# A state-space and attention block on one core: TensorE folds two steps' states together in every second step

## The chip, the cores and the metric

The kernel runs on one core of one Trainium2 chip. The metric is device microseconds of a whole launch, lower is better. The profiler recorded one execution instruction by instruction. In this document PE is TensorE (matmuls), DVE is VectorE, ACT is ScalarE, POOL is GpSimd and SP is the queue that issues the DMAs.

## The reference

Input x is 4 sequences of 512 tokens with 256 channels. The first half is a state-space layer, the second an attention and MLP block on the 64 best scored tokens of each sequence. The part that matters here is the scan of the first half, shortened:

```python
deltaA  = exp(einsum('bld,dn->lbdn', delta, A))        # n = 16 states per channel
deltaBu = einsum('bld,bln->lbdn', delta * u, Bm)
def step(h, inp):
    dA, dBu, c = inp
    h = dA * h + dBu                                   # along the 512 tokens
    return h, einsum('bdn,bn->bd', h, c)               # sum over the 16 states
y   = scan(...) + u * D
out = (y * silu(r)) @ W_out + xs                       # r, xs, u, delta, Bm, C come from x
x1  = layernorm(x + out);  then scores, top 64 tokens, attention + MLP on them, layernorm
```

## The kernel before

The loop that the change touches has 64 **steps**, t = 0 to 63: 16 for each of the 4 sequences (b = t // 16). A step takes one pair of 64-channel halves for two of the 16 states. Its work goes through five engines, which run their own programs and meet at semaphores:

- ACT `make_z` (L1009) multiplies delta times u by B, in four chunks of tokens for each two steps: chunks 0 to 2 are written in an even step for the next two, chunk 3 at the start of the following odd step. ACT `make_decay` (L1019) makes the decays.
- PE `turn_bu` (L522) transposes a quarter of that into one of three banks: four matmuls a call, two calls a step. I call them the first and the second turn of a step. PE issues the turns of step t+1 while it is in its own step t. The first turn of an even step reads newly made chunks, so it waits for ACT's chunk 3; this wait falls into PE's odd steps.
- DVE `scan` (L1171) runs the recurrence, two scans a step, into `state`, which has room for four steps. The first scan of step t waits until step t-4 has been folded (`summed`).
- POOL `weigh` (L1545) multiplies the state by C.
- PE `add_states` (L657) is the **fold**: two 128x512 matmuls with the constant matrix `fold` that sum the two states of a step into bank 4 (even steps) or bank 5 (odd steps). It waits for `weighed`, and for the first fold of a sequence into a bank also for `y_taken`: DVE must have read the finished y out of that bank (L1223).

Around these, each step has pieces of the sequence after (**fronts**: transposes of x, convolution in four quarters `cv0a` to `cv1d`, gate `r0`/`r1`, `dt`, `bc`, `cr`/`dl`, `du`) and of the sequence before (**tails**: `o0`, `o1`, scores `sb`, ranks, selection `pf`, gather `ga`, angles `cs`). The tables `FRONT_AT` and `TAIL_AT` say in which step each piece stands, on all engines. PE's order in a step is: first turn of t+1, fold, tails, second turn of t+1, fronts. ACT copies the result of many pieces out of PSUM and waits for them in its own order: `dt` (in steps with t%16 = 4) and the last convolution quarters stand in even steps, `r0`, `r1` (t%16 = 3), `bc` (5), `o0` (3), `du` (13) and `cs` (t = 47) in odd steps.

Of the kernel before, what the change touches and what calls it, by code (L numbers as in the profile page):

```python
# [90 lines left out]
def block_kernel(nc, x, W_in, conv_w, conv_b, W_x, W_dt, b_dt, A_log, D, W_out, w_router, wq, bq, wk, bk, wv, bv,  # L91
# [45 lines left out]
    def tails(t):  # L137

        b, n = t // NST, t % NST
        return [(b - 1, piece) for piece in TAIL_AT.get(n, ())] if b >= 1 else []  # L140

    def fronts(t):


        late = {"cv1b": -16, "cv1c": -15, "cv1d": -14}
        return [(b, piece) for b in range(B - 1, 0, -1) for off in sorted(FRONT_AT) for piece in FRONT_AT[off]
                if b * NST + (late.get(piece, off) if b == 1 else off) == t and not (b == 1 and piece in EARLY)]

    def norms(t):

        return NORM_AT.get(t - (B - 1) * NST)
# [47 lines left out]
    with ExitStack() as ctx:  # L199
# [320 lines left out]
        def _(pe):  # L520
# [114 lines left out]
            def turn_bu(u):  # L635

                g, k = u // 4, u % 4
                if u >= NBU:
                    pe.wait_ge(scanned, u - NBU + 1)
                for c in range(C):  # L640
                    if k == 0:
                        if g == 0 and c >= C // 2:
                            pe.wait_ge(z_dve, 2 * (c - C // 2 + 1))
                        else:
                            pe.wait_ge(z_act, z_count(g, c))
                    mm = turn(bank[BU_BANK[u % NBU]][:, c * P:(c + 1) * P],
                              zed[:, g % NZ, c, k].rearrange("p n d -> p (n d)"))
                mm.then_inc(bu_filled, 1)

            def add_states(t):  # L650

                b, m, h = t // NST, t % NST // 2, t % 2
                if m == 0 and b >= 1:
                    pe.wait_ge(y_taken, KD * (b - 1) + h + 1)
                pe.wait_ge(weighed, t + 1)
                for j in range(2):
                    mm = pe.matmul(bank[Y_BANK[h]][j * P // 2:(j + 1) * P // 2, :], fold[:], state[:, t % NH, j, :],  # L657
                                   start=(m == 0), stop=(m == NPAIR - 1))
                mm.then_inc(summed, 1)

            def rows_to_T(name, count):

                p = name[1]
                wait_free(pe, name)
                pe.wait_ge(h_ready, count)
                for k in range(KD):
                    mm = turn(at(name)[:, k * P:(k + 1) * P], h_rows[:, p, k * P:(k + 1) * P])
                fill_done(name, mm)
# [68 lines left out]
            for t in range(B * NST):  # L737
                if 2 * t + 2 < NU:
                    turn_bu(2 * t + 2)
                if t >= 2:  # L740
                    add_states(t - 2)
                for b, piece in tails(t):
                    tail(b, piece)
                if 2 * t + 3 < NU:
                    turn_bu(2 * t + 3)
                for b, piece in fronts(t):
                    front(b, piece)
                if norms(t) == "ht":
                    rows_to_T(("h1T", 0), 1)
# [907 lines left out]
```

## Time and profile before

| what | us |
|---|---|
| median of 3 runs (lowest, highest) | 519.88 (516.26, 520.61) |
| the profiled execution's own time | 519.67 |
| its span, first to last instruction | 517.9 |
| its loop of 64 steps on DVE, start of the first scan to the last | 62.9 to 368.4 |

The span and the time of the execution differ by 1.8 us, which lies outside of the recorded instructions. Busy shares of the span are PE 82%, ACT 65%, DVE 58% and POOL 49%, so no engine is full, and the loop is some three fifths of the span.

### The profile page before, as it was taken

The page shows a single profiled execution, that of the slowest core. Times are in us where ns is not written, and L with a number is a line of the kernel's source. Part 1 is how long each engine was busy: PE and PEld are TensorE (multiplying, and loading weights), DVE is VectorE, ACT ScalarE, POOL GpSimd, SP SyncE. Part 2 cuts the span into 40 slices and gives each one's busy share as a digit, 9 for nine tenths or more (in the row PEclk, how much of TensorE's full clock was granted, in tenths as well). Part 3 has the DMA queues.
Part 4 walks back from the last instruction along what each step waited for, and adds up shares of the span by engine and source line. Part 5 has one row for each costly group of instructions (what it writes and reads, how often), then busy time and mean ns, then how long its engine had stood idle before and what let it go on. Part 6 is the DMA issues. An engine that isn't in the chain of part 4 may idle for free.

```text
span 517.9 us, 6511 instructions
## 1 busy us (share of the span) xinstructions
PE 426.4 (82%) x2021; PEld 255.3 (49%) x2021; DVE 299.1 (58%) x600; ACT 334.5 (65%) x736; POOL 253.7 (49%) x230
## 2 busy tenths in 40 slices
PE   5988888878979869888958688877796888999992
PEld 3432443343445334544524454533384576887881
DVE  0301554558564549855655986789668257553365
ACT  4235689795769795577797386996186298543242
POOL 2001074469555659557667757695654144332012
PEclk9998999989999979899997697989998799999997
DMA  8001700104100102301000412662120000000003
GB/s 249 13 0 46 197 25 22 41 1 120 45 22 20 41 2 51 96 28 34 20 21 2 124 41 103 209 234 107 50 113 1 2 0 1 1 2 1 1 33 130
DMA packets 18710, 29.11 MB, mean 56 GB/s; under 512 B 2698, under 2 KB 10676, under 8 KB 18420
## 3 DMA queue, kind: packets, MB, share of 16 engines
q1 hardware_dynamic: 18676, 28.70, 17.8%
q8 instruction: 16, 0.26, 0.2%
q14 instruction: 18, 0.15, 0.1%
HBM read 22.27 MB, written 2.23 MB: 47 GB/s over the span
## 4 chain that ended last, share of the span: by engine, by line
PE 36%; ACT 15%; issue 9%; DVE 8%; POOL 7%; POOLq 0%; DVEq 0%; ACTq 0%
PE bank L522 6%; ACT loop_buf L1009 6%; PE bank L657 5%; POOL state L1545 4%; PE bank L538 4%; ACT front_a L1019 3%; PE bank L833 3%; DVE state L1171 3%; PE bank L809 3%; PE bank L603 2%; ACT state L1043 2%; ACT state L1044 1%; PE bank L841 1%; PE bank L800 1%; PE bank L612 1%
## 5 line engine op out<-in xcount | busy, mean ns | idle before, releaser
L1171 DVE TENSOR_TENSOR_SCAN state<-front_a,bank 128x512 f32<-128x512 f32 x128 | 151.2, 1209 | 102.2 <-PE bank L522 62.3
L522 PE MATMUL bank<-ident,loop_buf 128*128 128x128 f32 x512 | 90.9, 299 | 40.1 <-ACT loop_buf L1009 33.3
L522 PEld LDWEIGHTS bank<-ident,loop_buf 128*128 128x128 f32 x512 | 63.0, 149 | 109.5 <-issue 37.3
L1009 ACT ACTIVATE loop_buf<-copy,b_rows 128x256 f32<-128x256 f32 x252 | 105.3, 496 | 0.1
L1545 POOL TENSOR_TENSOR state<-state,c_own 128x1024 f32<-128x1024 f32 x32 | 75.2, 2359 | 50.3 <-DVE state L1171 50.3
L1545 POOL TENSOR_TENSOR state<-state,front_a 128x1024 f32<-128x1024 f32 x32 | 79.9, 2510 | 37.9 <-DVE state L1171 37.9
L1019 ACT ACTIVATE front_a<-loop_buf,a_neg 128x512 f32<-128x512 f32 x128 | 84.4, 712 | 10.9 <-DVE state L1171 9.9
L657 PE MATMUL bank<-state,fold 128*64 128x512 f32 x256 | 75.5, 671 | 10.2 <-POOL state L1545 6.1
L538 PE MATMUL bank<-front_c,conv_raw 128*128 128x512 f32 x128 | 60.4, 603 | 2.9 <-ACT front_b L884 1.2
L538 PEld LDWEIGHTS bank<-front_c,conv_raw 128*128 128x128 f32 x128 | 22.9, 195 | 23.7 <-issue 20.4
L1562 POOL TENSOR_TENSOR loop_buf<-state 128x256 f32<-128x256 f32 x24 | 17.8, 742 | 30.3 <-DVE state L1316 30.3
L884 ACT ACTIVATE front_b<-bank,vec 128x512 f32<-128x512 f32 x16 | 10.9, 682 | 31.5 <-PE bank L538 28.4
L884 ACT ACTIVATE copy<-bank 128x512 f32<-128x512 f32 x20 | 11.4, 594 | 28.2 <-PE bank L522 20.6
L681 PE MATMUL bank<-h,copy 128*128 128x128 f32 x192 | 24.5, 280 | 3.2 <-DVE state L1312 2.3
L681 PEld LDWEIGHTS bank<-h,copy 128*128 128x128 f32 x192 | 22.5, 192 | 6.0 <-DVE state L1312 3.6
L1312 DVE SCALAR_TENSOR_TENSOR state<-bank,vec,cosT 128x128 f32<-128x128 f32 x48 | 14.5, 344 | 18.8 <-ACT state L1044 18.6
L1519 POOL TENSOR_TENSOR copy<-front_c,front_b 128x1024 f32<-128x1024 f32 x4 | 8.0, 1998 | 35.0 <-ACT front_b L884 35.0
L657 PEld LDWEIGHTS bank<-state,fold 128*64 128x64 f32 x256 | 13.5, 144 | 22.7 <-POOL state L1545 9.1
L1043 ACT ACTIVATE state<-bank,vec 64x128 f32<-64x128 f32 x48 | 17.4, 364 | 10.3 <-PE bank L681 9.5
L1189 DVE TENSOR_SCALAR front_c<-front_b 128x512 f32<-128x512 f32 x2 | 0.9, 429 | 32.2 <-ACT front_b L948 32.1
L1044 ACT ACTIVATE state<-bank,vec 64x128 f32<-64x128 f32 x48 | 17.3, 360 | 0.6
L603 PE MATMUL bank<-w_out_s,gT 128*128 128x256 f32 x64 | 17.1, 390 | 0.4 <-POOL gT L1574 0.4
(197 smaller groups left out, 681.6 us busy)
## 6 DMA issues: line engine op xcount, KB each, us to landing
front_a<-c_stage SPq DMA_DIRECT2D x32, 128.0 KB, 2.9
c_own<-c_stage SPq DMA_DIRECT2D x32, 128.0 KB, 2.9
loop_buf<-front_b SPq DMA_DIRECT2D x32, 128.0 KB, 2.4
copy<-in_L_attn_x SPq DMA_DIRECT2D x4, 512.0 KB, 4.9
front_b<-in_L_ffn_wo SPq DMA_DIRECT2D x1, 2048.0 KB, 9.0
copy<-in_L_ffn_wq SPq DMA_DIRECT2D x1, 2048.0 KB, 9.6
out<-loop_buf SPq DMA_DIRECT2D x3, 512.0 KB, 2.9
conv_raw<-in_L_attn_conv_w SPq DMA_DIRECT2D x2, 512.0 KB, 3.7
```

Source lines behind the costliest of these rows:

```text
L522: return pe.transpose(dst, src, ident[:])
L538: mm = pe.matmul(at(name)[:], conv_x[:, k, i, o * P:(o + 1) * P], xT[:, i, k:k + L], start=(j == 0), stop=(j == TAPS * KD - 1))
L603: mm = pe.matmul(t[:, i * DM:(i + 1) * DM], gT[:, k, cols], w_out_s[:, k, :], start=(k == 0), stop=(k == KD - 1))
L657: mm = pe.matmul(bank[Y_BANK[h]][j * P // 2:(j + 1) * P // 2, :], fold[:], state[:, t % NH, j, :], start=(m == 0), stop=(m == NPAIR - 1))
L681: mm = pe.matmul(at(name)[:, i * P:(i + 1) * P], w_qk[:, k, head * P:(head + 1) * P], hT[:, k, p * P:(p + 1) * P], start=(k == 0), stop=(k ...
L884: drain_done(name, act.activation(dst, at(name)[:] if src is None else src, func, **kw))
L1009: act.activation(zed[:, g % NZ, c, :, i, :], du_rows[b % 2][:, c, :].rearrange("p (k d) -> p k d", k=2 * KD), ACT.Copy, scale=b_rows[:, b ...
L1019: act.activation(decay[:, u % NDA, :], delta_wide[:, b % 2, k, :], ACT.Exp, scale=a_neg[:, k, m:m + 1]).then_inc(decay_made, 1)
L1043: act.activation(qk_swap[0:mid, i0 % NQK, i, :], src[mid:, :], ACT.Identity, bias=vec[mid:, w:w + 1])
L1044: last = act.activation(qk_swap[mid:, i0 % NQK, i, :], src[0:mid, :], ACT.Identity, bias=vec[0:mid, w:w + 1])
L1171: dve.tensor_tensor_scan(state[:, t % NH, j, :], decay[:, u % NDA, :], bank[BU_BANK[u % NBU]][:], 0.0, ALU.mult, ALU.add).then_inc(scanned, 1)
L1545: pool.tensor_tensor(state[:, t % NH], state[:, t % NH], c_wide[g % NCW].unsqueeze(1).to_broadcast([P, 2, L]), ALU.mult).then_inc(weighed, 1)
```

## The change

PE calls `add_states` in odd steps alone, twice: first for step t-3, then for step t-2. The fold of an odd step stays in the PE step where it was; the fold of an even step is issued one PE step later, in front of it. The two folds behind the loop (steps 62 and 63) stay. No other engine's program changes.

```diff
             for t in range(B * NST):
                 if 2 * t + 2 < NU:
                     turn_bu(2 * t + 2)
-                if t >= 2:
+                if t % 2 and t >= 3:
+                    add_states(t - 3)
                     add_states(t - 2)
                 for b, piece in tails(t):
                     tail(b, piece)
```

Below, on PE in steps 5 and 6 (the first turn of step 6, in bank 0, is the first row; `bc` is L569 and `dl` is L586). Before:

```order
L522 MATMUL bank0<-ident,loop_buf 128x128 x4
L657 MATMUL bank5<-state,fold 64x512 x2
L522 MATMUL bank2<-ident,loop_buf 128x128 x4
L569 MATMUL bank6<-copy1,w_x_s 32x512 x2
L522 MATMUL bank3<-ident,loop_buf 128x128 x4
L657 MATMUL bank4<-state,fold 64x512 x2
L522 MATMUL bank0<-ident,loop_buf 128x128 x4
L574 MATMUL bank7<-ident,bcT 128x32 x4
```

After:

```order
L522 MATMUL bank0<-ident,loop_buf 128x128 x4
L657 MATMUL bank4<-state,fold 64x512 x2
L657 MATMUL bank5<-state,fold 64x512 x2
L522 MATMUL bank2<-ident,loop_buf 128x128 x4
L569 MATMUL bank6<-copy1,w_x_s 32x512 x2
L522 MATMUL bank3<-ident,loop_buf 128x128 x4
L522 MATMUL bank0<-ident,loop_buf 128x128 x4
L574 MATMUL bank7<-ident,bcT 128x32 x4
```

In the odd step two folds now stand between the first turn and everything behind it; in the even step none does. Next, on PE in steps 18 to 20, where the first folds of the second sequence stand (L603 and L607 are `o0`, L560 are `r0` and `r1`). Before:

```order
L522 MATMUL bank3<-ident,loop_buf 128x128 x4
L657 MATMUL bank4<-state,fold 64x512 x2
L522 MATMUL bank0<-ident,loop_buf 128x128 x4
L522 MATMUL bank2<-ident,loop_buf 128x128 x4
L657 MATMUL bank5<-state,fold 64x512 x2
L603 MATMUL bank6<-w_out_s,gT 128x256 x2
```

After:

```order
L522 MATMUL bank0<-ident,loop_buf 128x128 x4
L522 MATMUL bank2<-ident,loop_buf 128x128 x4
L657 MATMUL bank4<-state,fold 64x512 x2
L657 MATMUL bank5<-state,fold 64x512 x2
L603 MATMUL bank6<-w_out_s,gT 128x256 x2
```

The fold of step 16 (bank 4) now stands behind the second turn of step 19 and the first turn of step 20.

## Rows read from the trace of the kernel before

**Rows 1.** The page: span, and PE's busy time.

```profile
span 517.9 us, 6511 instructions
PE 426.4 (82%) x2021; PEld 255.3 (49%) x2021; DVE 299.1 (58%) x600; ACT 334.5 (65%) x736; POOL 253.7 (49%) x230
```

**Rows 2.** Busy time by stage, the loop: PE, PEld, DVE, ACT, POOL, then granted clock.

```profile
62.00:373.00 311.00, 256.19 (x1134) 131.80 (x1132) 206.43 (x287) 230.85 (x457) 203.23 (x124) 0.93 0.20 62
```

**Rows 3.** Who waited for whom, whole span: us in total, times, longest.

```profile
DVE state L1171 <- PE bank L522: 62.3, 36, 4.2
...
DVE state L1171 <- ACT front_a L1019: 35.7, 13, 5.0
...
PE bank L522 <- ACT loop_buf L1009: 33.3, 37, 3.4
...
PE bank L657 <- POOL state L1545: 6.1, 4, 2.8
...
PE bank L657 <- DVE gT L1223: 4.1, 3, 1.5
```

**Rows 4.** Groups of instructions: the folds.

```profile
L657 PE MATMUL bank<-state,fold 128*64 128x512 f32 x256 | 75.5, 671 | 10.2 <-POOL state L1545 6.1 <-DVE gT L1223 4.1
```

**Rows 5.** Timeline, steps 4 and 5: start, duration, instruction, idle before and releaser.

```profile
82.66 1.08 PE L657 MATMUL bank<-state,fold 128*64 128x512 f32 x4
...
87.87 0.57 ACT L884 ACTIVATE dtT<-bank 128x512 f32<-128x512 f32 x1
...
89.29 0.33 PE L522 MATMUL bank<-ident,loop_buf 128*128 128x128 f32 x1 [0.95 <-ACT loop_buf L1009]
89.55 1.08 PE L657 MATMUL bank<-state,fold 128*64 128x512 f32 x4
...
89.94 2.54 DVE L1171 TENSOR_TENSOR_SCAN state<-front_a,bank 128x512 f32<-128x512 f32 x2 [2.56 <-PE bank L522]
90.56 0.66 PE L522 MATMUL bank<-ident,loop_buf 128*128 128x128 f32 x4
91.15 1.90 PE L569 MATMUL bank<-copy,w_x_s 128*32 128x512 f32 x4
...
93.17 0.59 ACT L884 ACTIVATE bcT<-bank 32x512 f32<-32x512 f32 x1 [2.71 <-PE bank L569]
```

**Rows 6.** Timeline, step 12: DVE, and PE's second turn of step 13.

```profile
122.06 4.54 DVE L1171 TENSOR_TENSOR_SCAN state<-front_a,bank 128x512 f32<-128x512 f32 x4
...
123.32 0.66 PE L522 MATMUL bank<-ident,loop_buf 128*128 128x128 f32 x4 [0.32 <-DVE state L1171]
```

**Rows 7.** Timeline, steps 13 to 15: ACT's copies of `du`, PE's first turn of step 16.

```profile
131.45 1.09 ACT L884 ACTIVATE copy<-bank 128x512 f32<-128x512 f32 x2 [2.95 <-PE bank L522]
...
136.98 0.33 PE L522 MATMUL bank<-ident,loop_buf 128*128 128x128 f32 x1 [0.47 <-ACT loop_buf L1009]
```

**Rows 8.** Timeline, steps 18 and 19: the fold of step 16, ACT's copy of `o0`.

```profile
149.89 1.08 PE L657 MATMUL bank<-state,fold 128*64 128x512 f32 x4 [1.51 <-DVE gT L1223]
...
155.85 0.60 ACT L884 ACTIVATE z<-bank 128x512 f32<-128x512 f32 x1 [3.02 <-PE bank L607]
```

**Rows 9.** Timeline, steps 20 to 23: `dt` and `bc` on ACT, PE's first turn of 24.

```profile
166.14 0.60 ACT L884 ACTIVATE dtT<-bank 128x512 f32<-128x512 f32 x1 [0.24 <-PE bank L566]
...
171.47 0.59 ACT L884 ACTIVATE bcT<-bank 32x512 f32<-32x512 f32 x1 [2.71 <-PE bank L569]
...
178.58 0.33 PE L522 MATMUL bank<-ident,loop_buf 128*128 128x128 f32 x1 [1.30 <-ACT loop_buf L1009]
```

**Rows 10.** Timeline, steps 47 to 53: PE's first turns, ACT's copies of `cs` and `o1`.

```profile
304.11 0.33 PE L522 MATMUL bank<-ident,loop_buf 128*128 128x128 f32 x1 [0.85 <-ACT loop_buf L1009]
...
307.46 0.28 ACT L995 ACTIVATE cosT<-bank 128x128 f32<-128x128 f32 x1 [2.18 <-PE bank L631]
...
312.36 0.33 PE L522 MATMUL bank<-ident,loop_buf 128*128 128x128 f32 x1 [0.47 <-ACT loop_buf L1009]
...
329.19 0.60 ACT L884 ACTIVATE z<-bank 128x512 f32<-128x512 f32 x1 [0.49 <-PE bank L607]
```

## The prediction, written before the changed kernel ran

> **What bounds the kernel now.** I read the page first: 517.9 us of span, PE busy for 426.4 of them and no engine full [rows 1]. The changed code lies in the loop of 64 steps, so I then took the stretch of the loop: 311 us with PE busy 256, ACT 231, DVE 206, POOL 203 [rows 2]. With four engines at two thirds to four fifths, what counts is who waits for whom. The list of waits says it [rows 3]: the scans on DVE wait for PE's turns (62.3 us) and for ACT's decays (35.7), and PE's turns wait for ACT's chunks of z (33.3 us in 37 places). The folds, which the change moves, themselves wait little: 6.1 us for POOL in 4 places and 4.1 for DVE's reading of y in 3. So the loop is a ring of PE and ACT: PE finishes a piece, ACT copies it out, ACT makes chunk 3 of z behind it, PE's first turn of the next even step waits for that chunk. The third reading is the timeline around each such wait, since only the order of instructions tells whether a fold stands in the idle time of PE or on the ring.
>
> **The price of one fold.** The folds of a step start at 89.55 and the next turn starts at 90.56 [rows 5]: 1.0 us of PE, called F below. The group of all folds, 75.5 us for 64 steps [rows 4], gives 1.18 each, with the stretches at a lower granted clock in it; that is F's upper bound, 1.0 its lower. No instruction is added or taken away, and no DMA or SP wait is touched.
>
> **What the move does, as lags.** I call L the lag of the new PE program behind the old one right after the fold of an odd step, where both have issued the same set of folds. In the even step that follows the new program has no fold, so behind the place of the old fold its lag is L-1 (in units of F), until the next odd step's two folds bring it back to L. If PE is never idle in between, nothing is lost: the fold is repaid in the same pair of steps. If PE is idle before the first turn of an odd step because ACT's chunk 3 is late, it is different. Call ACT's own lag A. The turn ends with lag A, then come two folds where there was one, so L becomes A+1: the old even fold had stood in PE's idle time and cost nothing, and now stands on the ring. That alone is no loss either, since L-1 = A. It becomes one where ACT or DVE then waits for something that PE issues **in the odd half**, between the two folds and the next even fold's place. There A takes the value of L, and the next idle time adds another F. ACT lines up behind odd pieces at `r1`, `o0`, `bc`, `du` and `cs`, and behind even pieces at the convolution's ends, `dt` and `o1`. What looks like slack in one place is thus given back only if the ring passes through an even piece.
>
> Walking the timeline with this rule gives the sum.
> - Step 5: PE waits 0.95 us for the chunk; the fold of the step before at 82.66 was free, since ACT did not wait for `dt` (its copy at 87.87 shows no idle time). Then `bc` stands behind both folds, and ACT waits 2.71 us for it, so its lag follows in full [rows 5]. +1. The scan at 89.94, which started 0.3 us after the turn, now waits for the fold of step 2 as well, since it frees the state's slot: about 0.8 later, inside the same lag.
> - Step 7: the chunk wait again (the pattern of step 23 in rows 9), L = A+1 = 2.
> - Steps 12 and 13: DVE runs four scans without a break and PE's second turn of step 13, in an even step, waits 0.32 us for it [rows 6]. DVE's chain began with a second turn of an even step, issued in an odd one, so its lag is the full L = 2; the even step doesn't get its F back here. +1, L = 3.
> - Steps 13 to 15: ACT waits 2.95 us for `du`, an odd piece, so A = L = 3, it then works without a break, and PE waits for chunks (0.47 us for the last one) [rows 7]. +1, L = 4.
> - Step 18: here the change gains. PE waits 1.51 us until DVE has taken y, and only then folds step 16 [rows 8]. In the new order two turns (0.6 us each, by the starts 90.56 and 91.15 in rows 5) fill that wait, and both folds follow it. So PE reaches `o0`, for which ACT waits 3.02 us, earlier by the two turns, 1.1 us, counted as 1. -1, L = 3 and A = 3.
> - Steps 20 and 21: ACT waited just 0.24 us for `dt` [rows 9], so ACT's lag falls by 0.24 only, not by 1; then `bc` is again behind both folds with 2.71 us of waiting. +0.76.
> - Step 23: PE waits 1.30 us for the chunk [rows 9], the even fold before it was free. +1. The scores `sb` stand behind both folds, and DVE's chain of ranks and scans behind `sb`, so DVE and, through the decays, ACT take over this lag.
> - The third sequence repeats this: -1 (step 34), +0.76, +1. By now L is 5.5.
> - Steps 45 to 49: ACT copies `du`, then PE waits 0.85 for the chunk in step 47: +1. ACT waits 2.18 us for `cs`, an odd piece, and PE then waits 0.47 for the last chunk: +1 [rows 10].
> - Step 50: the third wait for y, -1. Step 53: ACT waited 0.49 us for `o1`, an even piece [rows 10], so half of one F comes back and half is lost: +0.5.
> - Steps 54 to 63: ACT, then DVE's dense chain behind `sb` of step 57, carry the lag to the end. The last folds are where they were. The waits for POOL (6.1 us) lie before odd folds or beside DVE's chain and give nothing back.
>
> Sum: 1+1+1+1, -1+0.76+1, -1+0.76+1, +1+1-1+0.5 = **7.0 us**. On the profiled execution's own time, 519.67, that is **526.7 us**; that execution lies 0.2 us below the median of the runs. Behind the loop nothing changes, since each later stage waits for PE or DVE there. F at 1.18 would make it 8.3 us; if a third of the plus terms (9.0 us of them) does not add up, because another chain is later at that place, it is 4.
>
> **A rule against the row.** The granted clock of the loop is 0.93 [rows 2], so 7% x 2 x 311 = 43.5 us of it ran at 1.2 instead of 2.4 GHz. The Trainium skill, page "TensorE: Matmul & The Clock Gate", section "Loop structure matters more than you think", says that matmuls stay at full clock where they follow each other closely and drop where waits stand between them. By that page, gathering four fold matmuls in one burst would raise the clock. The row can't show it either way; the bursts get longer in odd steps and PE's idle time gets longer in even ones. It is the third rival.
>
> **The rivals.**
> (1) *Repaid in the pair.* PE alone is the ring, L stays 0, and only the y waits count: 3 x 1 us gained at most, 516.7 to 519.7 us. For it: PE is the busiest engine, and in the convolution steps it has no gap but the one for the chunk, whose copy waits for an even piece. Against it: 33.3 us of PE's waiting is for ACT, and the waits of 2.71 us on `bc`, an odd piece.
> (2) *The clock falls.* In even steps PE waits up to F longer for the chunk. If that turns a quarter more of the loop's slow time on (11 us, at PE's 82% busy share and half of the rate: 11 x 0.5 x 0.82 = 4.5 us), the time is 531.2. It decides only where these idle stretches set off the lower clock; in rows 9 and 10 PE's gaps before the chunk are 0.47 to 1.30 us.
> (3) *The clock rises, and the kernel gets faster.* Bursts of four folds, with one interruption of the turns less in every pair, take a quarter of the 43.5 us away: 4.5 us, with the y waits 3 us, 519.67 - 7.5 = 512.2 us. It needs that rival 1 holds and that the clock answers. Against it: each pair of steps keeps its wait for the chunk, which is where PE stands still, and that wait gets longer.
>
> **How the numbers follow.** Forecast 526.7 us with an own range of 521.5 to 531 (some of the plus terms fail, or F is 1.18 and a few slow stretches fall on the folds): chance 0.62. Rival 1: 0.20. Rival 2: 0.10. Rival 3: 0.08. A measurement of this kernel can tell about 1%, 5.2 us, from no change. Of the forecast's chance a bit over a quarter lies under 525.1, so same is 0.17 + 0.20 = 0.37, slower 0.45 + 0.10 = 0.55, faster 0.08. The range goes from 517 (most of rival 1) to 531.5 (half of rival 2), and leaves out rival 3 and the ends of the other two.
>
> **What the new profile would show.** If I am right: the folds' 256 matmuls stand in 31 bursts of 8 and the last two of 4; the fold's waits for y (4.1 us) are gone; PE's waits for ACT's chunks are more in total than 33.3 us, since PE arrives earlier at them; ACT's copy of `bc` in step 5 is about 1 us later against the start of the loop, and the copy of `cs` in step 47 about 6 us. First scans of even steps start about 1 us after the turn and not 0.3. If rival 1 is right, ACT's copies of `bc` and `du` keep their distance to the start of the loop. If the clock decides, the loop's granted clock leaves 0.93 by more than 0.01. The prediction would be wrong above all if ACT or DVE has slack at the odd pieces that I took for dense work, or if the clock's slow stretches, which lie at other places in the new run, swallow or double the lags.

## The result and the profile after

| | kernel before | changed kernel |
|---|---|---|
| first comparison: median of 4 executions each, us | 518.14 (516.26 to 520.61) | 527.64 (525.98 to 529.52) |
| ratio to before, 95% interval | | 1.0184 [1.0137, 1.0231] |
| measured again later: median of 28 and of 11, us | 520.72 (515.27 to 525.09) | 525.57 (521.85 to 530.09) |
| ratio to before, 95% interval | | 1.0103 [1.0067, 1.0139] |
| span of the profiled execution, us | 517.9 | 525.7 |

The changed kernel is slower by 1.0 to 1.8%, 5 to 10 us. The forecast was 526.7 us. Medians here are over all executions; ratios leave out executions over 1.5% longer than the fastest of their kernel, which is why the two differ for e8 and e11 below. Line numbers of the changed kernel are one higher behind the change (L1171 is now L1172).

The page of the changed kernel, span and first line of the busy times:

```profile
span 525.7 us, 6511 instructions
PE 426.8 (81%) x2021; PEld 255.4 (49%) x2021; DVE 298.4 (57%) x600; ACT 334.7 (64%) x736; POOL 253.1 (48%) x230
```

PE has the same 2021 matmuls and the same busy time (426.4 before), and 7.8 us more span: what was added is waiting. By stage (us from the start of the span), first the start of the loop and then the stretch of rows 2 (PE, PEld, DVE, ACT, POOL, granted clock):

```profile
62.00:122.00 60.00, 50.15 (x197) 23.87 (x199) 30.87 (x26) 49.55 (x94) 30.79 (x15) 0.89 0.11 36
...
62.00:373.00 311.00, 251.87 (x1109) 130.19 (x1109) 200.55 (x283) 230.49 (x456) 197.75 (x122) 0.91 0.20 62
```

The granted clock of the loop went from 0.93 [rows 2] to 0.91. For the first 60 us, the kernel before has this line:

```profile
62.00:122.00 60.00, 50.90 (x210) 23.79 (x210) 34.52 (x27) 52.38 (x100) 34.83 (x16) 0.97 0.14 42
```

So the clock fell most, from 0.97 to 0.89, in this first stretch (about steps 0 to 11), while PE was as busy as before (50.15 us for 50.90) and issued 13 matmuls fewer. The waits of the changed kernel (in total, times, longest), for comparison with rows 3:

```profile
DVE state L1172 <- PE bank L657: 51.8, 16, 6.7
...
PE bank L522 <- ACT loop_buf L1010: 34.8, 47, 1.7
...
DVE state L1172 <- ACT front_a L1020: 31.5, 10, 5.0
...
DVE state L1172 <- PE bank L522: 25.3, 19, 2.4
```

DVE's 62.3 us of waiting for turns are now 25.3 for turns and 51.8 for folds: the first scan of an even step is released by the fold that frees its state's slot. Taken alone this row accuses the state slots; run e3 below shows that they are only the last in line. PE's waits for ACT's chunks went up from 37 to 47 places. The group of the folds, against rows 4:

```profile
L657 PE MATMUL bank<-state,fold 128*64 128x512 f32 x256 | 79.3, 748 | 1.7 <-POOL state L1546 1.7
```

The waits for y are gone, the one for POOL shrank from 6.1 to 1.7, and still the folds take 3.8 us more busy time. Where, the timeline of step 5 shows, against rows 5:

```profile
88.23 0.57 ACT L885 ACTIVATE dtT<-bank 128x512 f32<-128x512 f32 x1
...
89.66 0.48 PE L522 MATMUL bank<-ident,loop_buf 128*128 128x128 f32 x1 [0.80 <-ACT loop_buf L1010]
90.06 3.68 PE L657 MATMUL bank<-state,fold 128*64 128x512 f32 x8
...
92.18 1.22 DVE L1172 TENSOR_TENSOR_SCAN state<-front_a,bank 128x512 f32<-128x512 f32 x1 [4.44 <-PE bank L657]
93.67 1.11 PE L522 MATMUL bank<-ident,loop_buf 128*128 128x128 f32 x4
...
96.89 0.59 ACT L885 ACTIVATE bcT<-bank 32x512 f32<-32x512 f32 x1 [6.06 <-PE bank L569]
```

ACT reaches its wait for `bc` as before; the wait is 6.06 us and was 2.71. The chain of the prediction is there, only larger: the pair of folds took 3.68 us, since it ran at the lower clock.

To follow the lag through the loop, I took the start of the last matmul of each step's second turn in a profile, less that of the kernel before, less the shift of the loop's start (us, negative where a kernel is ahead of the kernel before; the forecast's L in the first row; the runs are described below):

| step | 6 | 8 | 10 | 16 | 24 | 32 | 40 | 48 | 58 | 63 |
|---|---|---|---|---|---|---|---|---|---|---|
| forecast | 1 | 2 | 2 | 4 | 4.8 | 4.8 | 5.5 | 6.5 | 7 | 7 |
| changed kernel | 2.8 | 6.3 | 2.9 | 6.6 | 10.3 | 6.9 | 10.3 | 7.7 | 7.2 | 7.1 |
| e9, the changed kernel again | 2.7 | 6.5 | 2.9 | 5.1 | 7.7 | 5.5 | 8.1 | 6.4 | 6.5 | 8.0 |
| e4, changed kernel with fillers | 0.5 | 3.2 | 0.4 | 3.9 | 7.0 | 4.2 | 7.1 | 5.4 | 4.4 | 6.4 |
| e5, the even fold ahead of the turn | -0.2 | 1.6 | 0.4 | 0.4 | -1.1 | -1.6 | -3.2 | -3.2 | -7.2 | -5.5 |
| e8, change up to step 17 | 2.7 | 6.5 | 2.9 | 6.2 | 6.5 | 6.5 | 6.5 | 6.5 | 6.5 | 6.5 |
| e11, e8 with fillers | 0.5 | 3.2 | 1.7 | 6.3 | 7.2 | 4.9 | 4.9 | 4.9 | 3.9 | 3.9 |
| e10, change from step 19 on | 0 | 0 | 0 | 0 | 3.7 | 0.1 | 6.0 | 4.1 | 3.9 | 6.0 |

The lag rises at the predicted places but overshoots, and falls again behind steps 8, 24 and 40, which the forecast had not. Each row is one execution. The two of the same changed kernel differ by up to 2.6 us in these columns (step 24), so smaller differences between rows say little.

One more thing moves the times. The first scan starts 63.6 us into the span in the changed kernel's profile and 58.0 us in that of e9, the same kernel. The two executions took 527.4 and 521.9 us; their loops, first scan to last, took 312.6 and 312.9 (305.4 in the kernel before). So the 5.6 us between these two times all stand ahead of the loop. A lag in the loop can therefore be compared between profiles better than whole times can.

### The profile page after: what moved, and what is told of

It reads as the page before. It is cut to its first block, busy times and chain, and to the rows that moved or that the text cites. A ratio compares the mean times of both kernels' runs of the same rounds, so it can differ in the third digit from the quotient of the medians.

```text
span 525.7 us, 6511 instructions
## 1 busy us (share of the span) xinstructions
PE 426.8 (81%) x2021; PEld 255.4 (49%) x2021; DVE 298.4 (57%) x600; ACT 334.7 (64%) x736; POOL 253.1 (48%) x230
## 4 chain that ended last, share of the span: by engine, by line
PE 29%; ACT 16%; issue 12%; DVE 11%; POOL 8%; DVEq 0%; POOLq 0%; ACTq 0%
ACT loop_buf L1010 6%; POOL state L1546 5%; DVE state L1172 4%; PE bank L657 4%; PE bank L522 4%; ACT front_a L1020 4%; PE bank L834 3%; PE bank L810 2%; ACT state L1044 2%; PE bank L538 2%; PE bank L603 1%; ACT state L1045 1%; PE bank L625 1%; PE bank L842 1%; PE bank L801 1%
## 5 line engine op out<-in xcount | busy, mean ns | idle before, releaser
L1172 DVE TENSOR_TENSOR_SCAN state<-front_a,bank 128x512 f32<-128x512 f32 x128 | 150.3, 1207 | 109.8 <-PE bank L657 51.8
L522 PE MATMUL bank<-ident,loop_buf 128*128 128x128 f32 x512 | 87.9, 294 | 47.5 <-ACT loop_buf L1010 34.8
L522 PEld LDWEIGHTS bank<-ident,loop_buf 128*128 128x128 f32 x512 | 61.4, 146 | 104.1 <-ACT loop_buf L1010 40.2
L657 PE MATMUL bank<-state,fold 128*64 128x512 f32 x256 | 79.3, 748 | 1.7 <-POOL state L1546 1.7
L657 PEld LDWEIGHTS bank<-state,fold 128*64 128x64 f32 x256 | 18.3, 162 | 33.4 <-issue 25.1
L885 ACT ACTIVATE copy<-bank 128x512 f32<-128x512 f32 x20 | 11.5, 595 | 26.9 <-PE bank L522 18.3
L1575 POOL TENSOR_TENSOR gT<-gT,copy 128x512 f32<-128x512 f32 x8 | 10.0, 1275 | 16.1 <-DVE gT L1224 16.1
```

Of the source, the lines that this page charges most:

```text
L522: return pe.transpose(dst, src, ident[:])
L885: drain_done(name, act.activation(dst, at(name)[:] if src is None else src, func, **kw))
L1172: dve.tensor_tensor_scan(state[:, t % NH, j, :], decay[:, u % NDA, :], bank[BU_BANK[u % NBU]][:], 0.0, ALU.mult, ALU.add).then_inc(scanned, 1)
```

## The experiments

The runs were measured in three groups, each on a chip of its own, with the kernel before in each of them. Its median was 515.8 us with e1 to e4, 519.3 with e5 to e8 and 520.7 with e9 to e12, so runs of different groups are compared by ratio. Even ratios carry some of this: that of the changed kernel was 1.0184 at first and 1.0103 with e9 to e12.

**e1, both folds ahead of the first turn.**

```diff
-                if 2 * t + 2 < NU:
-                    turn_bu(2 * t + 2)
                 if t % 2 and t >= 3:
                     add_states(t - 3)
                     add_states(t - 2)
+                if 2 * t + 2 < NU:
+                    turn_bu(2 * t + 2)
```

> Both folds of the pair stand ahead of the first turn of the odd step instead of behind it; all else as in the changed kernel. Ring theory (the loss comes from the even fold standing between the wait for ACT's chunk and the pieces that ACT then waits for): both folds now lie in PE's idle time before the chunk, PE reaches the odd pieces one fold earlier than in the kernel before, so 510 to 518 us, and ACT's wait for bc in step 5 under 2.7 us. Rival, pairs as such are the cost (two steps' folds in one burst hold up PE, wherever it stands): 525 to 529 us.

500.84 us, ratio 0.9705 [0.966, 0.975], a gain some 9 us larger than the best that I had expected. The same two folds in the same PE step, moved by one turn, are worth 4 to 5% against the changed kernel. In step 5 only the second turn now stands between PE's first turn and `bc` (the x5 are the last chunk and the second turn), and ACT's wait for it is 1.54 us, where it was 2.71 before and 6.06 in the changed kernel:

```profile
85.03 0.76 PE L522 MATMUL bank<-ident,loop_buf 128*128 128x128 f32 x5 [0.95 <-ACT loop_buf L1010]
...
85.73 1.90 PE L569 MATMUL bank<-copy,w_x_s 128*32 128x512 f32 x4
...
87.75 0.59 ACT L885 ACTIVATE bcT<-bank 32x512 f32<-32x512 f32 x1 [1.54 <-PE bank L569]
```

Its list of waits has PE waiting much less for ACT's chunks (12.4 us for 34.8), and something for POOL in exchange, since a fold ahead of the turn asks earlier for the weighed state:

```profile
PE bank L522 <- ACT loop_buf L1010: 12.4, 17, 2.7
PE bank L657 <- POOL state L1546: 11.5, 6, 3.4
```

The rival that a burst of folds is bad wherever it stands is out. The clock is not behind the gain either: over its loop the granted clock was 0.92, no higher than before (0.93).

**e2, the pairs in even steps.**

```diff
-                if t % 2 and t >= 3:
-                    add_states(t - 3)
+                if t % 2 == 0 and t >= 2:
+                    if t >= 4:
+                        add_states(t - 3)
                     add_states(t - 2)
```

(with the fold of step 61 added behind the loop)

> The pairs are issued in even steps (folds of steps t-3 and t-2 behind the first turn of an even step), so the odd steps, in which PE waits for ACT's chunk 3, have no fold behind that wait. Ring theory: PE reaches the odd pieces r1, bc, du, cs a fold earlier, so not slower than before, 512 to 519 us. Rival, late release of state slots: an odd step's scan now waits for the fold four steps back as the even one did, so 525 us or more. Rival, pairs as such: 525 to 529 us.

507.48 us, 0.9838 [0.977, 0.9906]. Faster than my whole expected range, and against both rivals. Here an odd step's scan waits for a fold four steps back, in the same way as the even one's in the changed kernel (DVE waits 11.6 us for folds in 8 places), without harm.

**e3, five state slots in the changed kernel.**

```diff
-        NDA, NBU, NH, NZ, NCW = 4, 3, 4, 2, 4
+        NDA, NBU, NH, NZ, NCW = 4, 3, 5, 2, 4
```

(cut: `bcT`, `cosT` and `sinT` also get new places, to make room)

> The changed kernel with room for five steps' states instead of four (bcT, cosT and sinT share memory with tensors that are used at other times), so the first scan of an even step no longer waits for the fold of four steps back. Slot theory (DVE's 51.8 us of waiting for folds in the new trace is the loss): 517 to 520 us. Ring theory: DVE's wait goes over to PE's second turn or ACT's decays, 524.5 to 528 us.

527.85 us, 1.0237 [1.0182, 1.0292]. DVE's waiting for folds is gone from its list of waits, and all of it stands in the row for turns:

```profile
DVE state L1172 <- PE bank L522: 81.0, 43, 4.8
...
PE bank L522 <- ACT loop_buf L1010: 37.4, 48, 2.2
```

The slot theory fell: 51.8 + 25.3 us have become 81.0. A releaser named by the profile is the one that came last; it need not be the one that counts.

**e4, fillers in PE's idle time in the changed kernel.** The fillers compute nothing that is used; the real transposes overwrite them.

```diff
                 for c in range(C):
+                    if u in FILL_U:      # first turns of steps 6, 8, 10, 24, 26, 40, 42, 58
+                        for _ in range(6 if c == 0 else 3):
+                            turn(bank[BU_BANK[u % NBU]][:, c * P:(c + 1) * P], ident[:])
```

> The changed kernel with 15 extra transposes of the identity matrix (0.13 us each, overwritten by the real ones) in the first turns of steps 6, 8, 10, 24, 26, 40, 42 and 58: 6 ahead of the wait for chunk 0, 3 ahead of each of the others, where PE stands idle. Clock theory (in steps 5 to 9 the longer idle time brought the granted clock down, and the two folds took 3.7 us instead of 1.9): the folds of steps 5 and 7 are back at 1.9 us, the granted clock of the loop rises from 0.91 to 0.94 or more, and the time falls to 520 to 524 us. Ring theory without the clock: 527 us or a little more, since the fillers only take time.

522.43 us, 1.0116 [1.0065, 1.0168]: 120 more matmuls and a smaller ratio than e3 (1.0237), which has the changed kernel's program on PE and ran beside it, and than the changed kernel in the first comparison; against its second one the difference is inside the intervals. The profile is clearer. The folds of step 5 take 1.94 us again, and of step 7 too:

```profile
84.29 1.94 PE L661 MATMUL bank<-state,fold 128*64 128x512 f32 x8
...
97.94 1.94 PE L661 MATMUL bank<-state,fold 128*64 128x512 f32 x8
```

and the granted clock of the first stretch and of the loop are

```profile
62.00:122.00 60.00, 52.10 (x247) 28.74 (x245) 36.47 (x29) 48.13 (x93) 37.24 (x17) 0.97 0.14 36
...
62.00:373.00 311.00, 259.90 (x1233) 146.11 (x1231) 206.26 (x285) 226.14 (x449) 201.69 (x124) 0.93 0.19 58
```

In step 5 the fillers bring back 2.2 of 2.8 us of lag, and 2 to 3 us in most of the loop (table). At its end 0.7 to 1.2 us of that is left: the loop, from the first scan to the last, took 311.4 us for 312.6. This is the clock's share less what the fillers cost. In step 7 they cost much: a stretch at the lower clock lay on the fillers themselves, six of them took 1.49 us, and PE had no wait left there, so step 7 is no clean test. The expected 0.94 of the loop was not reached, but 0.93 is what the kernel before has, and at that clock the loop is still 6.0 us longer than before. So the lower clock is not the main part of the loss.

**e5, only the even fold ahead of the turn.**

```diff
                 if t % 2 and t >= 3:
                     add_states(t - 3)
+                if 2 * t + 2 < NU:
+                    turn_bu(2 * t + 2)
+                if t % 2 and t >= 3:
                     add_states(t - 2)
```

(in place of the turn ahead of both)

> As the changed kernel, but the fold of step t-3 stands ahead of the odd step's first turn, and the fold of t-2 behind it as ever. If the place of the even fold behind the chunk wait is the whole loss, this is no slower than the kernel before, 510 to 517 us, since even pieces come a fold earlier and odd pieces where they were. Rival, folding late (three steps after instead of two) costs by itself: 520 us or more.

513.03 us, 0.9872 [0.9811, 0.9933]. It differs from the changed kernel in nothing but the even fold's place on one side of the turn or the other, and goes from slower to 1.3% faster than before. This is the test of the prediction's main step. By step 16 the lag is 0.4 us, where the changed kernel has 5.1 to 6.6 (table). The clock doesn't explain it: it was 0.92 over the loop. It even worked against e5 in step 5, where the fold behind the turn and what follows ran at the lower clock and ACT's wait for `bc` grew to 4.29 us:

```profile
85.22 1.71 PE L657 MATMUL bank<-state,fold 128*64 128x512 f32 x4
...
90.43 0.59 ACT L886 ACTIVATE bcT<-bank 32x512 f32<-32x512 f32 x1 [4.29 <-PE bank L569]
```

Folding the even steps three steps late shows no cost by itself.

**e6, the kernel before with only the odd fold ahead, and e7, with every fold ahead, unpaired.**

```diff
 # e6
+                if t % 2 and t >= 3:
+                    add_states(t - 2)
                 if 2 * t + 2 < NU:
                     turn_bu(2 * t + 2)
-                if t >= 2:
+                if t % 2 == 0 and t >= 2:
                     add_states(t - 2)
 # e7
+                if t >= 2:
+                    add_states(t - 2)
                 if 2 * t + 2 < NU:
                     turn_bu(2 * t + 2)
-                if t >= 2:
-                    add_states(t - 2)
```

> The kernel before, with the fold of each odd step moved ahead of the first turn and nothing paired. Ring theory: it takes the odd fold off the ring, most of the gain of the run with both folds ahead (501 us), so 501 to 508 us. Rival, the gain of that run came from the pair: 513 to 517 us.

> The kernel before with every fold ahead of its step's first turn, unpaired. Ring theory: 500 to 507 us; if pairing adds something of its own, it is the difference to 501 us. Rival, pairs are what gains: 513 us or more.

e6: 510.25 us, 0.9816 [0.9744, 0.9889]. e7: 510.75 us, 0.9826 [0.9757, 0.9895]. Both are faster than before. Both missed my numbers in us (501 to 508 and 500 to 507), but as ratios to the 515.8 us of e1's group those ranges are 0.971 to 0.985 and 0.969 to 0.983, and both lie inside. They stand 1.1 and 1.2% above e1's 0.9705. So the place ahead of the turn gives 1.7 to 1.8%, and pairing seems to give another 1.2% once the pair stands there. That rests on two groups of runs, between which the changed kernel's ratio moved by 0.8%, so its size is not shown. The loops of the profiles, 289.5 us in e1 and 300.1 in e7, point the same way. Part of it is in the fold's own group, first e1, then e7:

```profile
L657 PE MATMUL bank<-state,fold 128*64 128x512 f32 x256 | 67.2, 641 | 14.8 <-POOL state L1546 11.5 <-DVE gT L1224 3.3
```

```profile
L657 PE MATMUL bank<-state,fold 128*64 128x512 f32 x256 | 75.4, 670 | 24.2 <-POOL state L1545 15.4 <-DVE gT L1223 8.7
```

8.2 us less busy time, and 9.4 us less of waiting, of which 5.4 us for y. I had expected nothing certain of pairing.

**e8, the change in steps 0 to 17 alone.**

```diff
-                if t >= 2:
-                    add_states(t - 2)
+                if t < 18:
+                    if t % 2 and t >= 3:
+                        add_states(t - 3)
+                        add_states(t - 2)
+                else:
+                    add_states(t - 2)
```

> The change in steps 0 to 17 alone, the rest as before. The lag in the new trace stands at 6 to 7 us after step 17 of 7.2 at the end, so if lags are carried along the ring, this has most of the loss: 520 to 524 us. Rival, the loss is spread over the loop and the lag is taken up by later slack: 516 to 518 us.

Median of ten executions 522.3 us (518.4 to 527.6), the profiled one at 526.8; ratio 1.004 [0.9999, 1.0082], so the times do not show that this part has most of the loss. The profile's row in the table has a lag of 6.2 us at step 16 and then 6.5, unchanged, in all of the 46 steps that are as before: in this execution no slack took the lag up. That is not so in general. The profiled execution is one of the three longest of the ten, and in e11 below, which has the same program from step 18 on, the lag falls from 7.2 us at step 24 to 3.9 at the end.

**e9 to e12** were measured together. e9 is the changed kernel unaltered.

> The changed kernel once more, beside the others of this call, so that its time and theirs are from one chip. 1.014 to 1.023 of the kernel before, as measured first.

525.57 us, 1.0103 [1.0067, 1.0139], below what was measured first and below my range (its upper end touches the lower end of the first interval). In its profile the pairs of folds of steps 5 and 7 take 3.68 us again, and the loop 312.9 us.

e10 has the change from step 19 on:

```diff
-                if t >= 2:
+                if t < 18:
+                    if t >= 2:
+                        add_states(t - 2)
+                elif t % 2:
+                    if t > 19:
+                        add_states(t - 3)
+                    add_states(t - 2)
+                elif t == 18:
                     add_states(t - 2)
```

> The change from step 19 on alone. The first-part run had a lag of 7 us in its profile but only 3 us in its median, so if the two parts add up to the whole change, this is 1.007 to 1.016 of before (4 to 8 us). Rival, read from the profile of the changed kernel, whose steps 18 to 63 last as long as before (227.6 against 227.3 us): no difference, 0.996 to 1.004.

525.99 us, 1.0099 [1.0058, 1.014]. The reading "steps 18 to 63 of the changed kernel last as long as before, so they cost nothing" was wrong. Alone they cost as much as the whole change measured beside them, and their lag (table) comes in steps 21 to 24, 37 to 40 and at the end. Already the second profile of the changed kernel (e9) gains 3.2 us of lag behind step 18, where the first gained 0.7. In the profiles the two parts do not add up: e8's loop is 6.5 us longer than before and e10's 5.5, first scan to last, and with both parts it is 7.1 to 7.4.

e11 is e8 with fillers (as in e4) in the first turns of steps 6 and 8 alone.

> The change in steps 0 to 17 alone, with 15 filler transposes of the identity in each of the first turns of steps 6 and 8, in PE's idle time. Clock theory for the spread of the first-part run (518.4 to 527.6 us): its slow executions are those in which the folds of steps 5 and 7 run at the lower clock; with fillers these go away, all executions lie at 516 to 521 us and the folds of step 5 take 1.9 us. Ring theory without the clock: median stays within 1.5 us of the first-part run, spread as wide.

Median of twelve executions 521.67 us (515.7 to 528.2), ratio 0.9992 [0.9947, 1.0036]. The spread did not shrink, so my explanation of it, the folds of steps 5 and 7, fell. The profile shows why fillers there can't end it: the folds of step 7 are at full clock, but those of step 9 are at the lower one, as the fold of step 9 is in the kernel before (1.98 us for 1.08).

```profile
102.01 1.94 PE L661 MATMUL bank<-state,fold 128*64 128x512 f32 x8
...
109.04 3.48 PE L661 MATMUL bank<-state,fold 128*64 128x512 f32 x8
```

e12 puts both folds inside the odd step's first turn, ahead of its last chunk (in `turn_bu`, with `folds` the two steps' numbers):

```diff
                 for c in range(C):
+                    if c == C - 1:
+                        for s in folds:
+                            add_states(s)
```

> Both folds stand inside the odd step's first turn, ahead of its last chunk, so that they fill the wait for chunk 3 itself and ask POOL for the weighed state a little later than in the run with both ahead of the turn. Ring theory: 0.965 to 0.975 of before, 1 to 4 us less than both ahead of the turn if POOL's 11.5 us of holding up folds shrinks; rival, folds so late push the last chunk's transpose behind them and back onto the ring: 0.978 to 0.99.

512.41 us, 0.987 [0.9822, 0.9917]. PE's waiting for POOL did shrink, from 11.5 to 4.4 us, but the time lies in the rival's range, and DVE waits 78.1 us for turns (62.4 in e1), as the rival's mechanism would have it. The best version stays e1.

## Why the prediction was right

**What bounds the loop.** Right: the ring of PE and ACT. PE's place in it decides 4 to 5% by the side of one turn on which two folds stand (changed kernel against e1), and DVE's and POOL's waits follow.

**The even fold was free where PE waited for the chunk, and is now on the ring.** Right, and shown by e5, which moves only that fold to the front of the wait and ends at 0.9872, with a lag of 0.4 us at step 16. In step 5 of the changed kernel ACT's wait for `bc` grew from 2.71 to 6.06 us, by the fold and by the lower clock together; with the clock back at full there (e4) the lag grew by 0.8 us, one F. That the first scan waits for the fold was called "inside the same lag"; e3 shows it.

**The price F.** At full clock the second fold lengthens the burst by 0.86 us: pairs take 1.94 us where one takes 1.08. Two turns that now follow each other directly in even steps, with no fold between, take 1.16 us off, not 1.0. I had both at 1.0. The difference, 0.3 us for each pair of steps, comes back wherever PE alone carries the ring: the lag of the second turn is 6.90 in step 32 and 6.60 in step 34. This recovery was missing in the walk.

**The steps one by one.** Steps 5 and 7 were to add 1 us each and added 3.1 and 3.5, both with their folds at the lower clock; 3.4 of it was back by step 10, where the kernel before ran at the lower clock and the changed one did not. Steps 12 and 13 (the missing F because of DVE) can't be told from the recovery around them. Steps 15 to 23 and 37 to 39 rise as said and overshoot to 10.3 both times (the pairs of steps 23 and 39 took 3.59 and 3.68 us, again at the lower clock), then fall to 6.9 and 7.7. ACT's copies against the start of the loop: `bc` in step 5 came 3.1 us later, for 1 forecast, and `cs` in step 47 7.7 us later, for 6. Step 49's +1 did not last: the second turn of step 50, right behind its folds, has a lag of 9.6 us (6.9 in e9), that of step 52 has 6.9 (5.0). Between them the kernel before itself ran at the lower clock: its fold of step 48 took 1.98 us for 1.08.

**The wait for y.** Wrong, -1 each: nothing came back in step 18 (the second turns of steps 18 and 20 both have a lag of 6.46 us) or in step 34 (6.60 and 6.60). At the third wait, in step 50, the lag did fall, but the lower clock of the kernel before lies there. In step 18 the changed kernel's timeline is:

```profile
157.94 0.33 PE L522 MATMUL bank<-ident,loop_buf 128*128 128x128 f32 x1 [0.47 <-ACT loop_buf L1010]
158.19 1.94 PE L657 MATMUL bank<-state,fold 128*64 128x512 f32 x8
...
162.98 0.60 ACT L885 ACTIVATE z<-bank 128x512 f32<-128x512 f32 x1 [3.87 <-PE bank L607]
```

The wait for y [rows 8] was not turned into work. The first turn of step 20, which I had moved into it, needs ACT's chunks, and these came as late as y did. The wait has changed its name.

**The sum.** 7.0 us forecast, 7.1 (and 7.4 in e9) in the loop of the profiles, 5 to 10 in the medians. This closeness is luck: the clock made steps 5 and 7 dearer by 4.9 us (3.1 and 3.5 for 0.86 each) and gave 3.4 back by step 10, the 3 us for y were not gained, and the 0.3 us of each pair and the missing +1 worked the other way. The plus terms of the forecast also add up to 10.0 us and not to the 9.0 that stand there; the sum of 7.0 is right.

**The rivals.** Repaid in the pair: out as the whole, but there as the 0.3 us. The clock falls: by 0.02 over the loop and 0.08 in the first stretch, so the sign that I had named for this rival (more than 0.01) was there. It has a part in where the lag stands, and at step 5 e4 shows that the longer idle time does it, since extra matmuls in it take the lower clock away. It does not decide the time: with the loop at 0.93 again (e4) it is 6.0 us longer than before, and e5 and e1, with loops at 0.92, are 6.0 and 15.9 us shorter. The clock rises: out, since four folds in a row raised it neither in the changed kernel (0.91) nor in e1 (0.92). The rule of the Trainium skill, page "TensorE: Matmul & The Clock Gate", section "Loop structure matters more than you think" (matmuls that follow closely keep the clock, waits between them lose it), agrees with step 5 in its second half: the gap that the even fold had been filling got longer (0.47 to 1.63 us), and the folds behind it ran at 1.2 GHz.

**What stays open.** Why single executions of e8 and e11 spread over 9 and 12 us, while the four of e1 lie within 1.3 us. There are two candidates, different places of the lower clock and the start of the loop, which moved by 5.6 us between the two profiles of the changed kernel; with one profile of each run neither can be tied to the spread. Why the start moves is not known. How much pairing is worth is open too, and how the loss divides among the steps, since the table's rows of one and the same kernel differ by up to 2.6 us.

## What to carry to other kernels

Before moving work on an in-order engine, ask on which side of that engine's own wait it stands. Work just ahead of a wait for another engine is free as far as it fits into the wait and its own inputs are there (e1's folds waited 11.5 us for POOL); the same work just behind it delays everybody who waits next. Here the kernel with the pair of folds behind one turn is 1.0 to 1.8% slower than the kernel before, and with the pair ahead of it 3.0% faster.

In these runs pairing the folds paid, if at all, only once their place was right. And a wait list names the last releaser: remove it once, as with the fifth slot, before believing it.

## What the runs showed of the hardware that I had not expected

- Four fold matmuls in a row take 1.94 us at full clock, two take 1.08, and two turns in direct succession save another 0.15 over the fold taken out between them (1.16 for 1.01): in these rows each change between turns and folds costs PE about 0.15 us.
- An idle stretch of PE that grew from 0.47 to 1.63 us at the head of step 5's first turn goes with a new stretch at 1.2 GHz over the folds behind it, 3.68 us for 1.94. Extra matmuls in that idle time, whose results are not used, took the low clock away there (e4, e11); in both, the next stretch at the lower clock lay on the fillers of step 7. How much idle time it takes is not shown: in e5 the four waits of that turn were 0.62, 0.41, 0.47 and 0.95 us, for 0.47, 0.41, 0.47 and 0.95 before, and the fold behind them took 1.71 us for 1.08.
- The first scan starts between 58.0 and 63.6 us in two profiles of the changed kernel (e9 and the first). That is nearly as much as the change's whole effect, and the reason to compare stretches of the loop and not ends of spans.
